# Layer 2's second value sweep: two of eight one-hots and the weight copy on GpSimd

## The chip, the cores and the metric

One Trainium2 chip; the kernel is one program on one core. The metric is device time in microseconds: 5602.24 us, the median of 3 runs (5601.0 to 5603.31).

## What is computed

Four graph layers run on 3125 nodes of 128 features and 50000 edges that are sorted by target. The change touches the third one (its code name is L2), and there only the last step of its second attention convolution. Cut to that:

```python
alpha = jnp.einsum('ehc,ehc->eh', q[dst], k[src]) / jnp.sqrt(jnp.float32(C))   # H=2 heads, C=128
p = jnp.exp(alpha - amax[dst])
denom = jax.ops.segment_sum(p, dst, num_segments=n) + 1e-16
out = jax.ops.segment_sum(p[:, :, None] * v[src], dst, num_segments=n)
out = out / denom[:, :, None]
out = out.mean(axis=1)          # mean of the two heads
return out + x @ Ws + bs
```

The softmax weights are known before the step begins (`alpha` in the kernel holds weight over denominator, halved for the mean). So each edge e has to add alpha[e,0] * v0[src] + alpha[e,1] * v1[src] to the row of its target node.

## The kernel before

Edges lie in tiles of 128, one edge to a partition. There are T = 416 tiles; each belongs to one block of 128 target nodes. Eight tiles (HU = 8) make a half, four halves (S4 = 4) an iteration, 13 iterations (G) a sweep: 52 halves. `half_no(i, h)` numbers them, m in what follows. `each_half` runs a function over all halves inside a loop of 13 iterations on one engine.

The sum over edges is a matmul: for each tile a one-hot matrix (128 edges by 128 nodes, 1 where the edge's target is that node) is the weight operand, the 128 mixed value rows are the moving operand, and the product is added to the node block's place in PSUM. `rec[1][:, tile, 1]` holds each edge's target inside its block, `iota_f` the numbers 0 to 127; comparing the two gives the one-hot.

The sweep is called L2F, "values mixed". Its data is already in DRAM, in the order of the edges (`rows_v2`, two heads side by side, 256 floats an edge). Each engine runs its own program, tied by counting semaphores:

- SyncE, `values_in` (L607 to L611): when a quarter of the ring is free (`ring_free`, given by TensorE), it issues one 1 MB transfer of eight tiles into `ring256`. Four halves fit in the ring.
- VectorE, `mix` (L1475 to L1487): copies the two softmax weights of the half's edges into `relw` (L1480), multiplies head 1's values by their weight (L1482), makes the eight one-hots in one instruction of 128x1024 into one of two slots of `ohv` (L1484, shown by the profile as L965, the helper's line), and adds head 0's scaled values (L1487). The one-hots of half m wait until TensorE is done with half m-2, whose slot they take; the add waits for ScalarE.
- ScalarE, `scale_l2f` (L1712 to L1720): waits for the weights in `relw`, then scales head 0's values tile by tile, eight instructions a half.
- TensorE, `sums_f` (L2143 to L2153): loads eight block numbers into registers, waits for the one-hots and the mixed values, runs eight fp32 matmuls (each two records in the trace), waits for its own last one, and frees the quarter of the ring.
- GpSimd does nothing in this sweep. Ahead of it lie the gathers of the scores' sweep (L2D), behind it those of the last layer (L3), which wait for node rows that are written after the sweep.

The names in the change: `gate(s, n)` is GpSimd's wait, with one increment of a helper semaphore; `last_head` (L784 on) is a function of L2's first value sweep, L2C, in which GpSimd already makes a part of the one-hots, with `tensor_scalar` on 128x128 (L793), after two small copies into `relw` (L780, L781). VectorE's work in L2C is a one-hot instruction of 128x1024 a half (L965 again), products of 128x256 (L1366) and sums that read PSUM (L1378). Elsewhere in the kernel, in the sort of the edges, GpSimd's small copies (L674, L675) run beside VectorE's comparisons L860 and L851.

Of the kernel before, what the change touches and what calls it, by code (L numbers as in the profile page):

```python
# [25 lines left out]
def gnn_stack(nc, a, out):  # L26
    f32, bf16, i32 = mybir.dt.float32, mybir.dt.bfloat16, mybir.dt.int32
    ALU, ACT, AX = mybir.AluOpType, mybir.ActivationFunctionType, mybir.AxisListType.X
    ds = bass.ds
    x_in, src_in, dst_in, w_in = a["x"], a["src"], a["dst"], a["edge_weight"]  # L30

    P, F = 128, 128
# [21 lines left out]
    NG = J // HU  # L54
    NS = 5
    JQ = J // 4
    assert 0 < EP <= P and P * JM + EP * HU == E and CH * CB == NB and NG % NS == 0 and NG % 2 == 0 and G * U >= (E + NB * (P - 1)) // P

    ctx = ExitStack()
    with ctx:  # L60
# [272 lines left out]
        def ph(name):  # L333
            if name not in made:
                made[name] = sem(name)
            return made[name]
# [29 lines left out]
        def half_no(i, h):  # L366
            return i * S4 + h
# [39 lines left out]
        def tiles_of(i, h):  # L407
            return ds(i * U + h * HU, HU)

        def each_half(eng, half):  # L410

            with eng.Fori(0, G) as i:
                for h in range(S4):
                    half(i, h)
# [228 lines left out]
        def _(pool):  # L643
# [16 lines left out]
            def gate(s, n):  # L660
                pool.wait_ge(s, n)
                pool.sem_inc(s_gate, 1)
# [138 lines left out]
                last_head(G - 1, h, (G - 1, h + 1) if h < S4 - 1 else None)  # L801
            gate(ph("node_rows"), ROWS["n2b"] + 16 * CH)
            gathers("L2D", 1, t_kv, 512, None)
            gate(ph("node_rows"), ROWS["n3"] + 16 * CH)
            gathers("L3", 1, t_h3, F, ring)

        @block.vector
        def _(dve):
# [666 lines left out]
            def mix(i, h):  # L1475

                s = h % 2
                m = half_no(i, h)
                v = ring256[:, h * HU:(h + 1) * HU, F:2 * F]
                V.tensor_copy(relw[:, s, :, 1:3], alpha[:, tiles_of(i, h), 0:2]).then_inc(ph("L2F_weights"), 1)  # L1480
                dve.wait_ge(s_rows[h], values_reloaded(i, h))
                V.tensor_tensor(v, v, alpha[:, tiles_of(i, h), 1:2].to_broadcast([P, HU, F]), ALU.mult).then_inc(ph("L2F_mixed"), 1)  # L1482
                dve.wait_ge(ph("L2F_product"), m + 1)
                one_hots(ohv[:, s * HU:(s + 1) * HU, :], 1, i, h).then_inc(ph("L2F_onehot"), 1)  # L1484
                dve.wait_ge(ph("L2F_mixed"), 2 * m + 1)
                dve.wait_ge(ph("L2F_scaled"), m * HU + HU)
                V.tensor_tensor(v, v, ring256[:, h * HU:(h + 1) * HU, 0:F], ALU.add).then_inc(ph("L2F_mixed"), 1)  # L1487

            each_half(dve, mix)
# [40 lines left out]
        def _(act):  # L1530
# [181 lines left out]
            def scale_l2f(i, h):  # L1712

                s = h % 2
                m = half_no(i, h)
                act.wait_ge(ph("L2F_weights"), m + 1)
                act.wait_ge(s_rows[h], values_reloaded(i, h))
                for k in range(HU):
                    v = ring256[:, h * HU + k, 0:F]
                    A.activation(v, v, ACT.Copy, scale=relw[:, s, k, 1:2]).then_inc(ph("L2F_scaled"), 1)  # L1720

            each_half(act, scale_l2f)

            root("n3")
# [13 lines left out]
        def _(pe):  # L1738
# [404 lines left out]
            def sums_f(i, h):  # L2143
                m = half_no(i, h)
                blocks = blocks_of(1, i, h)
                pe.wait_ge(ph("L2F_onehot"), m + 1)
                pe.wait_ge(ph("L2F_mixed"), 2 * m + 2)
                for k in range(HU):
                    last = M.matmul(psum_blocks[:, ds(blocks[k], 1), :], ohv[:, (h % 2) * HU + k, :],  # L2149
                                    ring256[:, h * HU + k, F:2 * F].unsqueeze(1), start=False, stop=False)  # L2150
                last.then_inc(ph("L2F_product"), 1)
                pe.wait_ge(ph("L2F_product"), m + 3)
                pe.sem_inc(ph("ring_free"), 1)  # L2153
# [58 lines left out]
```

## Time and profile before

| | |
|---|---|
| median of 3 runs | 5602.24 us |
| lowest, highest | 5601.0, 5603.31 us |
| the profiled execution | 5603.99 us |
| its span, first to last instruction | 5602.3 us |
| mean granted TensorE clock | 0.726 |
| busy, whole kernel: TensorE, VectorE, ScalarE, GpSimd | 3034.5, 3058.7, 961.0, 3701.8 us |
| the sweep L2F | about 4787 to 4999 us after the start, 212 us |

The profile shows for each engine when it was busy and what released it from a wait. A granted clock of 1.00 is 2.4 GHz and 0.50 is 1.2 GHz; a value between is a mean over a stretch. Only the sweep L2F is changed, so the views below are of that stretch, and of the places where the added kind of work already runs.

### The profile page before, as it was taken

Reading aid. Unit: us, or ns where it says so; the run is one execution under the profiler, and the core shown is the slowest. Engines: PE = TensorE matmul, PEld = TensorE weight load, DVE = VectorE, ACT = ScalarE, POOL = GpSimd, SP = SyncE. Lnnn points to the kernel's source line nnn. Section 1 sums busy time; section 2 is a strip of 40 time slices with the busy share of each in tenths; the row PEclk is TensorE's granted clock in tenths of the full one; section 3 lists DMA queues with packets and bytes.
Section 4 is the critical chain, followed back from the end, with each engine's and each line's share of the span. In section 5 each row is a group of like instructions: output and inputs, shape, how many; then the busy total and the mean of one; then the engine's idle time right before and its main releaser. Section 6 shows DMA issues by size and latency. Waiting matters only on the chain.

```text
span 5602.3 us, 75577 instructions
## 1 busy us (share of the span) xinstructions
PE 3034.5 (54%) x17159; PEld 2186.4 (39%) x17160; DVE 3058.7 (55%) x6436; ACT 961.0 (17%) x3599; POOL 3701.8 (66%) x4254
## 2 busy tenths in 40 slices
PE   3443377753333660144457776688896665544334
PEld 2333266653333660143433332233354433443333
DVE  9888622232223684133349888888516666881111
ACT  1121000000001000000015554577400000550000
POOL 1788777767777777777747775577416776007775
PEclk9999955555555555555579999899997777776556
DMA  2212112221112670133334444122128999552222
GB/s 56 67 27 53 52 52 52 52 42 26 27 26 16 102 107 13 37 82 80 81 59 129 130 128 122 38 60 60 32 87 266 342 330 309 197 173 53 52 52 52
DMA packets 292233, 520.85 MB, mean 93 GB/s; under 512 B 88170, under 2 KB 161120, under 8 KB 285408
## 3 DMA queue, kind: packets, MB, share of 16 engines
q1 hardware_dynamic: 166440, 284.29, 17.9%
q0 software_dynamic: 125728, 235.82, 17.2%
q8 instruction: 26, 0.43, 0.0%
q14 instruction: 39, 0.32, 0.0%
HBM read 418.05 MB, written 101.80 MB: 93 GB/s over the span
## 4 chain that ended last, share of the span: by engine, by line
POOL 45%; issue 30%; DVE 11%; PE 8%; DVEq 2%; ACT 2%; DMA 1%; POOLq 1%; ACTq 0%; SPq 0%; PEldq 0%
POOL work L719 30%; POOL rec_by_dst L679 6%; POOL rec_by_src L679 4%; PE ps L2086 3%; DVE acc L1378 3%; POOL acc L719 2%; POOL idx_slot L713 1%; ACT work L1720 1%; PE ps L1883 1%; PE ps L2149 1%; PE ps L2124 1%; PE ps L2073 1%; DVE work L860 1%; DVEq L403 1%; DVE work L909 1%
## 5 line engine op out<-in xcount | busy, mean ns | idle before, releaser
L1823 PE MATMUL ps<-work 128*128 128x128 f32 (+1 forms) x2496 | 705.0, 445 | 681.6 <-DMA work<-t_v,idx_slot 354.3
L719 POOL DMA_INDIRECT work<-t_h,idx_slot x832 | 799.0, 960 | 240.1 <-issue 221.7
L719 POOL DMA_INDIRECT work<-t_v,idx_slot x832 | 789.8, 949 | 240.1 <-issue 221.6
L1823 PEld LDWEIGHTS ps<-work 128*128 128x128 f32 x2496 | 587.1, 330 | 705.4 <-issue 705.4
L679 POOL DMA_INDIRECT rec_by_src<-sc_rec_s,sc_idx x392 | 420.8, 1074 | 113.3 <-issue 104.2
L719 POOL DMA_INDIRECT work<-t_xl,idx_slot x416 | 413.0, 993 | 120.1 <-issue 111.0
L679 POOL DMA_INDIRECT rec_by_dst<-sc_rec_d,sc_idx x392 | 396.4, 1011 | 113.3 <-issue 104.6
L2051 PE MATMUL ps<-big,work 128*128 x832 | 389.6, 611 | 126.9 <-DVE work L1320 126.0
L2073 PE MATMUL ps<-work 128*128 128x512 f32 x832 | 390.2, 609 | 73.4 <-DVE work L1366 48.3
L2124 PE MATMUL ps<-big,work 128*128 x832 | 324.0, 548 | 194.5 <-DVE aS L1435 123.1
L975 DVE COPY relw<-rec_s 128x16 f32 x104 | 19.4, 186 | 723.6 <-PE ps L1823 723.1
L713 POOL COPY idx_slot<-rec_d 128x8 int32 (+1 forms) x208 | 47.0, 226 | 528.7 <-DMA t_h<-acc 359.3
L793 POOL TENSOR_SCALAR work<-iota_f,relw 128x128 f32<-128x128 f32 x312 | 306.0, 985 | 123.2 <-PE ps L2073 113.9
L1684 ACT ACTIVATE work<-work,relw 128x128 f32<-128x128 bf16 x1040 | 326.5, 389 | 133.8 <-DVE work L965 69.4
L2124 PEld LDWEIGHTS ps<-big,work 128*128 128x128 f32 x832 | 208.6, 270 | 309.6 <-issue 275.8
L1378 DVE TENSOR_TENSOR acc<-acc,ps 128x512 f32 x416 | 284.5, 684 | 47.0 <-DVE acc L1378 44.5
L2006 PE MATMUL ps<-work 128*128 128x128 f32 x832 | 196.1, 430 | 208.6 <-DVE work L1269 208.6
L1320 DVE TENSOR_TENSOR work<-ps,work 128x512 f32<-128x512 f32 x416 | 279.6, 683 | 51.2 <-DMA work<-t_h,idx_slot 47.7
L965 DVE TENSOR_TENSOR work<-rec_d,ps 128x1024 f32<-128x1024 f32 x52 | 63.4, 1222 | 433.6 <-PE ps L1823 433.0
L1822 PEld LDWEIGHTS ps<-one_column,work 128*128 128x128 f32 x832 | 224.9, 330 | 173.3 <-issue 173.3
L1667 ACT ACTIVATE work<-work 128x128 f32<-128x128 f32 x832 | 250.1, 301 | 243.1 <-DVE work L1320 243.1
L965 DVE TENSOR_TENSOR work<-rec_d,iota_f 128x1024 f32<-128x1024 f32 (+1 forms) x156 | 190.7, 1222 | 177.3 <-PE ps L2006 167.6
(415 smaller groups left out, 6589.8 us busy)
## 6 DMA issues: line engine op xcount, KB each, us to landing
work<-rows_of_v_by_position SPq DMA_DIRECT2D x52, 1024.0 KB
work<-relT_by_dst SPq DMA_DIRECT2D x156, 256.0 KB
rows_of_h_by_position<-work SPq DMA_DIRECT2D x52, 512.0 KB
work<-rows_of_h_by_position SPq DMA_DIRECT2D x52, 512.0 KB
rows_of_v_by_position<-work SPq DMA_DIRECT2D x26, 1024.0 KB
rows_of_v_by_position<-acc SPq DMA_DIRECT2D x26, 1024.0 KB
work<-t_v,idx_slot POOLq DMA_INDIRECT x832
work<-relT_by_src SPq DMA_DIRECT2D x52, 256.0 KB
```

The costliest lines, as they stand in the source:

```text
L679: nc.gpsimd.indirect_dma_start(rec_dram[o], bass.IndirectOffsetOnAxis(ap=sc_idx[:, h * HU + k:h * HU + k + 1], axis=0), sc_rec[o][:, h * H ...
L719: nc.gpsimd.indirect_dma_start(to, None, table, bass.IndirectOffsetOnAxis(ap=idx_slot[:, h * HU + k:h * HU + k + 1], axis=0)).then_inc(s_g ...
L793: nc.gpsimd.tensor_scalar(ohw[:, k % 4, 3 * P:4 * P], iota_f[:, :], relw[:, s, k, 0:1], relw[:, s, k, 4:5], ALU.is_equal, ALU.mult).then_i ...
L965: return V.tensor_tensor(out_t, rec[o][:, tiles_of(i, h), 1:2].to_broadcast([P, HU, P]), iota.unsqueeze(1).to_broadcast([P, HU, P]), ALU.i ...
L1320: V.tensor_tensor(prod[:, k % 4, :].rearrange("p (h c) -> p h c", h=4), q, g, ALU.mult).then_inc(sig("L2A", "_multiplied"), 1)
L1378: V.tensor_tensor(part, part, ps[:, k % 4, :].unsqueeze(1), ALU.add).then_inc(ph("L2C_added"), 1)
L1667: ins = A.activation(q, q, ACT.Copy, accum_out=aS[:, s * HU + k, hd:hd + 1])
L1684: ins = A.activation(ohw[:, k % 4, hd * P:(hd + 1) * P], ohm[:, s * HU + k, :], ACT.Copy, scale=relw[:, s, k, 1 + hd:2 + hd])
L1823: ins = M.matmul(psum_blocks[:, ds(b, 1), 0:width], oh[:, s, :], ring[:, h * HU + k, 0:width].unsqueeze(1), start=False, stop=False)
L2051: M.matmul(ps[:, k % 4, :].unsqueeze(1), ohT[:, s, k * P:(k + 1) * P], big[:, ds(blocks[k], 1), :], start=True, stop=True).then_inc(sig("L ...
L2073: M.matmul(ps[:, k % 4, :], ring[:, h * HU + k, :], ohw[:, k % 4, :], start=True, stop=True).then_inc(ph("L2C_product"), 1)
L2124: last = M.matmul(ps[:, k % 4, 0:256].unsqueeze(1), ohT[:, s, k * P:(k + 1) * P], q2[:, ds(blocks[k], 1), :], start=True, stop=True)
```

## The change

GpSimd gets a loop of its own for the sweep. Per half it copies the softmax weights of the next half into `relw[..., 1:3]` and two columns of target numbers into `relw[..., 0:1]`, once ScalarE is done with the half before and its own one-hots are done; then it makes the half's last two one-hots (tiles 6 and 7) one by one. VectorE no longer copies the weights and makes six one-hots instead of eight. TensorE waits for both. Two engines give themselves credits at the start, and the counts of the waits are shifted to match.

```diff
+    FEWER = HU - 2
...
+            def weights_l2f(i, h):
+                s = h % 2
+                nc.gpsimd.tensor_copy(relw[:, s, :, 1:3], alpha[:, tiles_of(i, h), 0:2]).then_inc(ph("L2F_weights"), 1)
+                nc.gpsimd.tensor_copy(relw[:, s, FEWER:HU, 0:1], rec[1][:, ds(i * U + h * HU + FEWER, HU - FEWER), 1:2]).then_inc(ph("L2F_weights"), 1)
+
+            def last_one_hots(i, h, nxt):
+                s = h % 2
+                m = half_no(i, h)
+                if nxt:
+                    gate(ph("L2F_scaled"), m * HU + HU)
+                    gate(ph("L2F_helped"), m * (HU - FEWER) + HU - FEWER)
+                    weights_l2f(*nxt)
+                gate(ph("L2F_weights"), m * 2 + 2)
+                gate(ph("L2F_product"), m + 1)
+                for k in range(FEWER, HU):
+                    nc.gpsimd.tensor_scalar(ohv[:, s * HU + k, :], iota_f[:, :], relw[:, s, k, 0:1], None, ALU.is_equal).then_inc(ph("L2F_helped"), 1)
+
+            gate(ph("sm_back"), 6)
+            pool.sem_inc(ph("L2F_helped"), HU - FEWER)
+            weights_l2f(0, 0)
+            with pool.Fori(0, G - 1) as i:
+                for h in range(S4):
+                    last_one_hots(i, h, (i, h + 1) if h < S4 - 1 else (i + 1, 0))
+            for h in range(S4):
+                last_one_hots(G - 1, h, (G - 1, h + 1) if h < S4 - 1 else None)
...
-                V.tensor_copy(relw[:, s, :, 1:3], alpha[:, tiles_of(i, h), 0:2]).then_inc(ph("L2F_weights"), 1)
...
-                one_hots(ohv[:, s * HU:(s + 1) * HU, :], 1, i, h).then_inc(ph("L2F_onehot"), 1)
+                V.tensor_tensor(ohv[:, s * HU:s * HU + FEWER, :], rec[1][:, ds(i * U + h * HU, FEWER), 1:2].to_broadcast([P, FEWER, P]),
+                                iota_f[:, :].unsqueeze(1).to_broadcast([P, FEWER, P]), ALU.is_equal).then_inc(ph("L2F_onehot"), 1)
...
-                dve.wait_ge(ph("L2F_scaled"), m * HU + HU)
+                dve.wait_ge(ph("L2F_scaled"), m * HU + 2 * HU)
...
-                act.wait_ge(ph("L2F_weights"), m + 1)
+                act.wait_ge(ph("L2F_weights"), m * 2 + 2)
...
+            act.sem_inc(ph("L2F_scaled"), HU)
...
                 pe.wait_ge(ph("L2F_onehot"), m + 1)
+                pe.wait_ge(ph("L2F_helped"), (m + 2) * (HU - FEWER))
                 pe.wait_ge(ph("L2F_mixed"), 2 * m + 2)
```

## Rows read from the trace of the kernel before

**Rows 1.** The page's busy tenths, 40 slices of 140 us; VectorE.

```profile
DVE  9888622232223684133349888888516666881111
```

**Rows 2.** Stretches: us, busy us of each engine, clock, DMA share, GB/s.

```profile
4787.00:4999.00 212.00, 130.99 (x840) 117.76 (x841) 186.33 (x208) 128.49 (x417) 0.00 (x0) 0.85 0.70 238
5100.00:5200.00 100.00, 36.48 (x158) 33.90 (x158) 12.22 (x10) 0.00 (x0) 77.31 (x90) 0.64 0.20 52
4849.00:4871.00 22.00, 12.28 (x96) 11.17 (x96) 20.47 (x24) 13.12 (x43) 0.00 (x0) 1.00 0.88 292
4907.00:4912.00 5.00, 3.52 (x17) 3.24 (x17) 4.21 (x5) 3.62 (x13) 0.00 (x0) 0.50 0.65 234
```

**Rows 3.** TensorE in order of time: start, duration, what, idle before and releaser.

```profile
4852.93 2.05 PE L2149 MATMUL ps<-work 128*128 128x128 f32 x16 [1.43 <-issue]
4856.84 2.05 PE L2149 MATMUL ps<-work 128*128 128x128 f32 x16 [1.86 <-issue]
...
4909.01 3.78 PE L2149 MATMUL ps<-work 128*128 128x128 f32 x16 [1.48 <-DVE work L965]
4914.19 2.05 PE L2149 MATMUL ps<-work 128*128 128x128 f32 x16 [1.41 <-DVE work L965]
```

**Rows 4.** VectorE in order of time, in the same stretch.

```profile
4909.02 1.23 DVE L1487 TENSOR_TENSOR work<-work 128x1024 f32<-128x1024 f32 x1
...
4912.94 1.23 DVE L965 TENSOR_TENSOR work<-rec_d,iota_f 128x1024 f32<-128x1024 f32 x1 [1.48 <-PE ps L2149]
4914.08 1.22 DVE L1487 TENSOR_TENSOR work<-work 128x1024 f32<-128x1024 f32 x1
4915.22 0.17 DVE L1480 COPY relw<-alpha 128x16 f32 x1
4915.30 1.22 DVE L1482 TENSOR_TENSOR work<-work,alpha 128x1024 f32<-128x1024 f32 x1
```

**Rows 5.** Groups by line, 4787 to 4999: busy us, mean ns, idle before, releasers.

```profile
L2149 PE MATMUL ps<-work 128*128 128x128 f32 x832 | 128.0, 317 | 80.6 <-DVE work L965 26.7 <-issue 24.3 <-DVE work L1482 23.1
L1720 ACT ACTIVATE work<-work,relw 128x128 f32<-128x128 f32 x416 | 127.2, 388 | 79.9 <-DVE relw L1480 79.9
...
L1487 DVE TENSOR_TENSOR work<-work 128x1024 f32<-128x1024 f32 x52 | 63.7, 1224 | 12.1 <-ACT work L1720 11.9
...
L1480 DVE COPY relw<-alpha 128x16 f32 x52 | 9.0, 172 | 1.5 <-ACT alpha L1630 1.5
```

**Rows 6.** GpSimd in L2C: its group by line, and the start in order of time.

```profile
L793 POOL TENSOR_SCALAR work<-iota_f,relw 128x128 f32<-128x128 f32 x312 | 306.0, 985 | 123.2 <-PE ps L2073 113.9 <-POOL relw L781 0.4
...
3540.87 0.20 POOL L780 COPY relw<-rec_d 128x8 f32<-128x8 f32 x1 [6.53 <-ACT alpha L1630]
3541.01 0.20 POOL L781 COPY relw<-alpha 128x32 f32<-128x32 f32 x1
...
3541.61 1.59 POOL L793 TENSOR_SCALAR work<-iota_f,relw 128x128 f32<-128x128 f32 x2 [0.40 <-POOL relw L781]
```

**Rows 7.** Order of time at three places where both engines read SBUF.

```profile
359.02 1.28 DVE L860 TENSOR_TENSOR work<-big,iota_f 128x1024 bf16<-128x1024 f32 x1
359.67 0.68 POOL L674 COPY sc_idx<-big 128x8 int32 x1
360.23 0.36 DVE L851 TENSOR_TENSOR work<-big 128x200 bf16<-128x200 f32 x1
...
3629.93 1.22 DVE L965 TENSOR_TENSOR work<-rec_d,iota_f 128x1024 bf16<-128x1024 f32 x1
3630.04 1.77 POOL L793 TENSOR_SCALAR work<-iota_f,relw 128x128 f32<-128x128 f32 x1
...
3634.55 0.79 POOL L793 TENSOR_SCALAR work<-iota_f,relw 128x128 f32<-128x128 f32 x1 [1.35 <-PE ps L2073]
...
3634.95 0.43 DVE L1366 TENSOR_TENSOR work<-work,relw 128x256 f32<-128x256 bf16 x1 [0.44 <-issue]
```

**Rows 8.** ScalarE's first scalings of the sweep.

```profile
4787.52 2.45 ACT L1720 ACTIVATE work<-work,relw 128x128 f32<-128x128 f32 x8 [0.63 <-DVE relw L1480]
```

## The prediction

> **What bounds the kernel now.** I read the busy tenths first: the sweep lies in the 35th and 36th slice, where VectorE shows 8 both times [rows 1]. That suggests VectorE as the bound. The table by stretches makes it exact: in the 212 us of the changed sweep VectorE is busy 186, TensorE 131, ScalarE 128, GpSimd 0, at a mean granted clock of 0.85 [rows 2]. The clock takes two levels here (1.00 and 0.50, that is 2.4 and 1.2 GHz), so 0.85 means about 30% of the stage at the lower one. The next view is TensorE in order of time. A half's 16 matmul records (8 fp32 matmuls) take 2.05 us at 1.00 and up to 3.78 at 0.50, and ahead of each half TensorE idles 1.41 to 1.48 us, every fourth time 1.86 [rows 3]. That gap is the key. At 4914.19 TensorE starts a half whose VectorE add ran from 4909.02 to 4910.25, and at 4912.94 VectorE itself had waited 1.48 us for TensorE [rows 3, 4]. So the gap is not a wait for data: TensorE waits for its own last matmul, loads eight block numbers (every fourth time after a loop branch) and only then asks for its operands. TensorE's least time for the stage is then its busy 128.0 us plus 13 x (1.41 + 1.41 + 1.43 + 1.86) = 79.4 us of gaps, and it shows 80.6 us of idle time [rows 3, 5]: some 1.2 us in 212 are waits for VectorE or ScalarE. **TensorE's own loop bounds the sweep**, 3.58 us a half at the full clock (2.05 + 79.4/52) and 5.2 to 5.3 at the lower. (128.0 - 52 x 2.05) / 1.73 gives 12.4 halves at 1.2 GHz and 39.6 at 2.4. VectorE is second: three instructions 1.14 us apart, the copy 0.08, and some 0.3 waiting for ScalarE (11.9 us in 40 times), 3.8 in all [rows 4, 5]. It takes longer than TensorE where the clock is 2.4 GHz and catches up where it is 1.2, as at 4912.94, where it waits for TensorE.
>
> **What the change takes from VectorE.** The copy of the weights goes: 0.172 us long, but the next instruction starts 0.08 after it [rows 4, 5]. The one-hots shrink from 128x1024 to 128x768. A 128x256 product (L1366) takes 0.43 us and the 128x1024 one-hots 1.22 [rows 7], so 256 elements are 0.26: 1.14 becomes 0.88 from start to start. ScalarE's weights no longer wait for VectorE's previous half, so the wait of 0.3 ahead of L1487 [rows 5] can go. VectorE falls from 3.8 to 1.14 + 0.88 + 1.14 = 3.16 a half. On the path this is worth only the share of the 1.2 us in which TensorE waits, since its 52 gaps stay: I book nothing. ScalarE's eight scalings (2.45 us a half [rows 8]) stay; its 79.9 us of idle time [rows 5] sits beside TensorE's loop.
>
> **What it gives to GpSimd.** Each half now has two small copies and two one-hots there. The same forms exist in L2C: copies of 0.20 us, 0.14 apart, then 0.40 to the first one-hot, and two one-hots in 1.59 [rows 6]. From the last one-hot to the next copies there are two more waits on semaphores, one of them for its own one-hots; no row has them, and between 0.1 and 0.4 (the nearest wait of that kind [rows 6]) I take 0.3. Alone, a half costs GpSimd 0.14 + 0.20 + 0.40 + 1.59 + 0.3 = 2.6 us, which TensorE's 3.58 would hide.
>
> It is not alone. A GpSimd one-hot that starts 0.11 us after VectorE's one-hots (L965, both inputs in SBUF) takes 1.77 us, against 0.79 for one that meets no such instruction at its start [rows 7]: it stands still until about 1.09 us after the start of VectorE's instruction. The mean over the 312 is 985 ns, although L2C's half has one such long instruction to six one-hots, for most of VectorE's work there (L1378) reads PSUM [rows 6]. Small copies stretch too: one takes 0.68 us behind L860, where one alone takes 0.20 [rows 6, 7]. VectorE gives up nearly nothing: that L860 takes 1.28 us, L965 of the same shape 1.22 [rows 7]. In this sweep all three VectorE instructions read twice from SBUF and stand back to back. They would cover 3.16 us of each half, the state in which a one-hot stands still.
>
> **GpSimd's time a half.** Lower bound 2.6, none blocked. If each of the four once stands behind a full instruction: one-hots 2 x 1.77, copies 2 x 0.68, the waits between them 0.7, 5.6. For the value between: with a half of T us, 3.16/T of it is covered, and a start inside waits 0.57 on average (half of 1.14), so T = 2.6 + 4 x 0.57 x 3.16/T, which gives T = 4.3. I take 4.3: in L2C, where fewer instructions block, blocked and free one-hots already mix (312 at 985 ns), and here blocking is denser. TensorE starts a half only with both GpSimd one-hots there, so halves at 2.4 GHz go from 3.58 to 4.3: 39.6 x 0.72 = +28 us. Those at 1.2 GHz (5.2) hide 4.3 and let GpSimd get ahead, 12 x 0.9 = 11 us at most; it can run only two halves ahead (two slots), so I take -8. The larger gap makes TensorE idler, and idler stretches have the lower clock: with TensorE busy 36% the clock is 0.64 in the sweep L3, with 62% it is 0.85 here [rows 2]. At 4.3 it would be busy some 55%. I let the halves at 1.2 GHz grow from 12 to 21: 9 x (5.2 - 4.3) = +8. Its bounds are 0 and 20 more of them, 0 to +18.
>
> **The other added parts.** ScalarE's first weights come from two GpSimd copies that start together with VectorE's first product instead of one VectorE copy ahead of it (scaling starts at 4787.52 [rows 8]): each copy behind one instruction, 1.3 + 1.1 at most, nothing at least; +2. ScalarE's later waits for weights have scalings queued behind them, for which only VectorE's add waits; the weights of a half are written one half early, so they are late only when GpSimd is. Behind TensorE's new wait stand the eight matmuls and the credit that frees a quarter of the ring, so the reloads of 1 MB start later. No DMA is added or moved; the reloads keep 0.88 of the DMA engines busy at TensorE's fastest pace [rows 2], and a slower pace relaxes that. GpSimd's queue holds nothing else until the gathers of L3, which wait for node rows made after the sweep. Two credits (one instruction each on ScalarE and GpSimd) are nothing.
>
> **A rule weighed against the rows.** VectorE's instruction that starts 0.40 us into a GpSimd one-hot is not held up: 0.43 us long, the one-hot 0.79 [rows 7]. So GpSimd seems to need the reading path only early in its instruction, and VectorE pays at most the 0.06 of L860. The Trainium skill, SBUF — State Buffer, "Who interferes with whom", says otherwise for this side: whichever of the two starts first has the shared pair for its whole instruction and the other stands still. It also says that a two-input VectorE instruction in SBUF contends with GpSimd's reads, which rows 7 bear out. By the first rule the engines would take turns, rival three.
>
> **Rivals.** (1) *Hidden, not slower.* GpSimd's waits fall where VectorE idles anyway: its three instructions fill 3.16 of at least 3.58 us. If GpSimd needs under 3.6 us a half on average (at most two of the four blocked, and briefly), TensorE's loop stays the bound: 5602 + 2 for the start - 1 for waits saved = 5603, give or take 7 for where the clock falls. For it: GpSimd works two halves ahead, and the stretches at 1.2 GHz refill that lead. Against: both engines are released by the same event, TensorE's end two halves back, and VectorE then runs three instructions in a row. It decides at 3.6 us. (2) *Starved.* No row shows a one-hot behind two such instructions in a row. If the 0.05 us between them is too short for its read of 128 elements, each one-hot waits for VectorE's next idle time: GpSimd's half is 3.16 + 1.59 + 0.7 = 5.4 us, TensorE's gaps grow by 1.8 at 2.4 GHz, 39.6 x 1.8 = +71, at 1.2 GHz +2, in all 5675. For it: the 0.68 us copy ended 0.12 after the next VectorE instruction began, so a small read just fits in between [rows 7]; one of 128 elements is larger. (3) *Turns.* GpSimd holds the path for its whole 0.79 us and VectorE waits: 3.16 + 1.59 + 0.34 = 5.1 a half, 52 x 5.1 = 265 for 128.0 + 80.6 = 209, +56: 5658. Against: the overlap at 3634.95 without delay. (4) *Faster.* TensorE's waits vanish and the clock stays up: at most 21.4 us (128.0 - 106.6) and the 1.2, 5580. Against: its gaps do not change. (5) *The change does nothing on its terms*, because GpSimd's one-hots come late in one iteration only; this is rival 1 with another name and has its time.
>
> **How the numbers follow.** The profiled execution took 5603.99 us with a span of 5602.3, the median of three is 5602.24; the sum of terms, 28 - 8 + 8 + 2 = +30, goes on the median: 5632. Chances: forecast (4.0 to 4.9 us a half, 5615 to 5655) 0.50; hidden 0.24; starved 0.15; turns 0.07; faster 0.04. A difference of 0.2%, 11 us, is about what a measurement of this kernel can tell from no change. So faster 0.04, same 0.24, slower 0.72. The range reaches from 5600, inside the hidden case, to 5664, which holds turns and the milder part of starved, and leaves out some 0.2. The likeliest case alone spans 5615 to 5655.
>
> **What would show it.** In the changed profile: GpSimd's one-hots between 0.79 and 1.8 us with a mean over 1.1; TensorE's gaps ahead of L2149's successor over 1.5 us and put down to GpSimd; VectorE's three instructions still 1.22, 0.95 and 1.22 long, with its idle time in waits for TensorE; a granted clock under 0.85 in the sweep; ScalarE's 80 us of waits for VectorE gone. A mean one-hot near 0.8 and gaps of 1.38 to 1.86 as before would prove the hidden case; VectorE's instructions stretched to 1.6 and more, turns; one-hots of over 2 us, starved. The prediction is wrong, too, if TensorE's gap turns out to have been a wait for VectorE after all: then the sweep shortens.

## The result, and the profile after

| | kernel before | changed kernel |
|---|---|---|
| median of 6 runs | 5602.77 us | 5626.39 us |
| lowest, highest | 5595.10, 5608.13 us | 5621.21, 5628.80 us |
| the profiled execution, its span | 5603.99, 5602.3 us | 5627.29, 5625.3 us |
| sweep, VectorE's first product to TensorE's last matmul | 211.1 us | 231.8 us |

The ratio is 1.0039, 95% interval 1.0028 to 1.005: by the ratio the change makes the kernel slower by 22 us, and the medians lie 23.6 us apart. The spans of the two profiled executions differ by 23.0 us. Of these 20.7 lie in the sweep, and 2.2 had gathered before it began (VectorE starts it at 4789.7 in place of 4787.4, and nothing ahead of it was changed).

First the sweep by line, as [rows 5] for the kernel before. Columns: busy us, mean ns of one, idle time before them, and what ended it.

```profile
L821 POOL TENSOR_SCALAR work<-iota_f,relw 128x128 f32<-128x128 f32 x104 | 147.3, 1425 | 12.4 <-PE ps L2178 11.9
L2178 PE MATMUL ps<-work 128*128 128x128 f32 x832 | 141.3, 339 | 87.9 <-DVE work L1510 60.4 <-POOL work L821 26.0 <-issue 1.5
...
L1747 ACT ACTIVATE work<-work,relw 128x128 f32<-128x128 f32 x416 | 126.2, 388 | 97.6 <-POOL relw L809 70.5 <-DMA work<-rows_of_v_by_position 27.1
L1508 DVE TENSOR_TENSOR work<-work,alpha 128x1024 f32<-128x1024 f32 x52 | 64.9, 1247 | 1.6 <-ACT alpha L1657 1.6
L1514 DVE TENSOR_TENSOR work<-work 128x1024 f32<-128x1024 f32 x52 | 64.1, 1232 | 4.5 <-ACT work L1747 3.7
L1510 DVE TENSOR_TENSOR work<-rec_d,iota_f 128x768 f32<-128x768 f32 x52 | 49.9, 959 | 50.6 <-PE ps L2178 50.6
L809 POOL COPY relw<-rec_d 128x2 f32 x48 | 32.7, 680 | 0.0
L808 POOL COPY relw<-alpha 128x16 f32 x48 | 21.3, 443 | 12.9 <-POOL work L821 12.3 <-issue 0.3 <-ACT work L1747 0.3
```

VectorE's one-hots fell from 1.22 to 0.96 us and its copy is gone, but it now idles 50.6 us for TensorE. TensorE (L2178 is the former L2149) shows both parts of the loss: 13.3 us more of matmuls, though they are the same 832, and 7 us more of idle time. The stretch by itself (us, busy us of TensorE, its weight loads, VectorE, ScalarE and GpSimd, then clock, DMA share, GB/s), against 0.85 for the clock in [rows 2]:

```profile
4789.00:5023.00 234.00, 144.78 (x843) 131.01 (x846) 171.90 (x156) 127.70 (x418) 202.30 (x208) 0.78 0.63 215
```

GpSimd, idle before, is now the busiest engine of the stage. TensorE in order of time, first its start and then one iteration of four halves (start, duration, what, idle before and what ended it):

```profile
4794.27 2.05 PE L2178 MATMUL ps<-work 128*128 128x128 f32 x16 [2.01 <-POOL work L821]
4800.73 3.77 PE L2178 MATMUL ps<-work 128*128 128x128 f32 x16 [4.41 <-POOL work L821]
...
4849.71 2.96 PE L2178 MATMUL ps<-work 128*128 128x128 f32 x16 [2.00 <-POOL work L821]
4854.14 3.62 PE L2178 MATMUL ps<-work 128*128 128x128 f32 x16 [1.48 <-DVE work L1510]
4859.27 2.05 PE L2178 MATMUL ps<-work 128*128 128x128 f32 x16 [1.50 <-DVE work L1510]
4862.79 2.05 PE L2178 MATMUL ps<-work 128*128 128x128 f32 x16 [1.48 <-DVE work L1510]
4866.84 3.01 PE L2178 MATMUL ps<-work 128*128 128x128 f32 x16 [2.00 <-POOL work L821]
```

One gap is a plain wait for GpSimd: 4.41 us ahead of the second half, where the kernel before has 1.78. The rest of the sweep looks almost as before. In an iteration's steady state the kernel before has gaps of about 1.49, 1.39, 1.41 and 1.88 us, the changed kernel of 1.50, 1.49, 1.50 and 1.98: three of the four are longer by 0.1, one is as it was. Only at halves 38 and 42 (counted from 0) is there another wait for GpSimd, of 0.35. The 26.0 us that the group puts down to GpSimd (12 times) are mostly TensorE's own loop, as at 4849.71, where e_wait below, without GpSimd, has the same 2.0; GpSimd's one-hots merely were the last operand to come. They came with little to spare, though: eight halves start only 0.4 us after GpSimd's last one-hot, and 0.24 is what it takes where TensorE really waits. What changed from iteration to iteration is the time of the matmuls. From one iteration's first matmul to the next one's, the kernel before takes 16.5 to 16.9 us eight times, 17.5 at the start and 14.3 to 14.4 in three iterations without a single half at 1.2 GHz. The changed kernel has 21.1 at the start, 19.3 once and 17.0 to 17.5 in the others: no iteration without halves at 1.2 GHz is left. TensorE's clock is at 1.2 GHz for 101.9 us of the sweep, before for 64.1.

GpSimd in order of time, first its second pair of one-hots and then two pairs that stand one iteration apart:

```profile
4795.76 4.73 POOL L821 TENSOR_SCALAR work<-iota_f,relw 128x128 f32<-128x128 f32 x2
...
4851.33 1.17 POOL L821 TENSOR_SCALAR work<-iota_f,relw 128x128 f32<-128x128 f32 x2
...
4868.50 1.17 POOL L821 TENSOR_SCALAR work<-iota_f,relw 128x128 f32<-128x128 f32 x2
```

And the view of that line: number, then shortest, median and longest in ns. One by one, 33 of the 104 took 0.6 us, 42 from 1.1 to 1.7 and 29 from 2.1 to 2.7.

```profile
L821 POOL TENSOR_SCALAR work<-iota_f,relw x104: 593/1328/2713, 4791.8 to 5017.0; 128x128 f32<-128x128 f32 x104
```

### The profile page after: what moved, and what is told of

Read it like the earlier page. It is cut to its first block, busy times and chain, and to the rows that moved or that the text cites. A ratio compares the mean times of both kernels' runs of the same rounds, so it can differ in the third digit from the quotient of the medians.

```text
span 5625.3 us, 76185 instructions
## 1 busy us (share of the span) xinstructions
PE 3049.1 (54%) x17150; PEld 2191.0 (39%) x17160; DVE 3041.6 (54%) x6384; ACT 960.1 (17%) x3599; POOL 3904.3 (69%) x4462
## 4 chain that ended last, share of the span: by engine, by line
POOL 46%; issue 30%; DVE 11%; PE 8%; DVEq 2%; DMA 2%; POOLq 1%; ACT 1%; SPq 0%; PEldq 0%; ACTq 0%
POOL work L720 30%; POOL rec_by_dst L680 6%; POOL rec_by_src L680 4%; PE ps L2114 3%; DVE acc L1405 3%; POOL acc L720 2%; PE ps L2178 2%; POOL idx_slot L714 1%; PE ps L1911 1%; POOL work L821 1%; DVE work L887 1%; PE ps L2101 1%; DVEq L404 1%; DVE work L936 1%; PE ps L2152 0%
## 5 line engine op out<-in xcount | busy, mean ns | idle before, releaser
L2079 PE MATMUL ps<-big,work 128*128 x832 | 390.9, 613 | 127.8 <-DVE work L1347 126.9
L2152 PEld LDWEIGHTS ps<-big,work 128*128 128x128 f32 x832 | 200.1, 263 | 314.5 <-issue 286.3
L2079 PEld LDWEIGHTS ps<-big,work 128*128 128x128 f32 x832 | 151.0, 191 | 329.6 <-issue 319.5
L1005 DVE TENSOR_SCALAR work<-ps,relw 128x128 f32<-128x128 f32 x832 | 274.3, 401 | 3.8
```

Source lines behind the costliest of these rows:

```text
L1005: last = V.tensor_scalar(oh[:, s * HU + k, :], iota_p, relw[:, s, k, 0:1], relw[:, s, k, 1:2], ALU.is_equal, ALU.mult)
L2079: M.matmul(ps[:, k % 4, :].unsqueeze(1), ohT[:, s, k * P:(k + 1) * P], big[:, ds(blocks[k], 1), :], start=True, stop=True).then_inc(sig("L ...
L2152: last = M.matmul(ps[:, k % 4, 0:256].unsqueeze(1), ohT[:, s, k * P:(k + 1) * P], q2[:, ds(blocks[k], 1), :], start=True, stop=True)
```

## Experiments

The kernels e_six, e_side, e_wait, e_side_wait, e_dvewait, e_one, e_again and e_early_one ran on two other chips, where the kernel before takes 7037 and 6988 us because other stages take longer; each ratio is to the kernel before on the same chip, and the sweep itself has its usual length there: on the first of them 210.7 and 210.4 us in e_side and e_six, against 211.1, on the second 232.8 in e_again, against 231.8. The table gives the sweep as above, the busy time of TensorE's matmuls, the 51 gaps between its halves, and the time in the sweep at 1.2 GHz. (What the sweep has beyond matmuls and gaps is the way to the first matmul, 3.9 to 4.7 us.) The ratio is of whole kernels over several executions. The other columns come from one profiled execution each; the repeat e_again is 1.0 us from the changed kernel, and the three kernels that hardly touch the sweep are within 1.0 us of the kernel before, so differences of 1 or 2 us tell nothing.

| kernel | ratio, 95% interval | sweep us | matmuls | gaps | at 1.2 GHz |
|---|---|---|---|---|---|
| before | | 211.1 | 128.0 | 79.1 | 64.1 |
| changed | 1.0039 [1.0028, 1.0050] | 231.8 | 141.3 | 85.9 | 101.9 |
| e_again | 1.0035 [1.0019, 1.0051] | 232.8 | 141.6 | 86.5 | 106.5 |
| e_six | 1.0003 [0.9992, 1.0015] | 210.4 | 127.6 | 78.9 | 63.0 |
| e_weights | 1.0001 [0.9992, 1.0010] | 212.1 | 129.7 | 78.5 | 68.4 |
| e_side | 0.9997 [0.9985, 1.0008] | 210.7 | 127.1 | 79.7 | 64.5 |
| e_wait | 1.0009 [1.0000, 1.0018] | 220.2 | 132.1 | 84.2 | 76.2 |
| e_side_wait | 1.0010 [0.9999, 1.0020] | 222.7 | 134.4 | 84.4 | 82.6 |
| e_one | 1.0021 [1.0009, 1.0032] | 222.3 | 134.1 | 84.1 | 81.5 |
| e_dvewait | 1.0030 [1.0019, 1.0041] | 227.7 | 139.4 | 83.5 | 98.1 |
| e_early | 0.9986 [0.9977, 0.9995] | 205.0 | 126.0 | 75.1 | 54.7 |
| e_early_after | 1.0032 [1.0020, 1.0044] | 225.9 | 134.3 | 87.0 | 79.6 |
| e_early_one | 0.9980 [0.9968, 0.9991] | 199.4 | 127.8 | 67.4 | 58.2 |
| e_early_weights | 0.9948 [0.9934, 0.9961] | 179.7 | 106.5 | 69.3 | 3.2 |

**Is VectorE's relief worth nothing?** e_six takes a quarter of VectorE's comparing away and gives it to nobody: VectorE makes six one-hots a half, and tiles 6 and 7 use one-hots made once ahead of the sweep, so a quarter of this step's sums is left out. e_weights moves only the copy of the weights to GpSimd, without a new wait on TensorE.

```diff
-                one_hots(ohv[:, s * HU:(s + 1) * HU, :], 1, i, h).then_inc(ph("L2F_onehot"), 1)
+                V.tensor_tensor(ohv[:, s * HU:s * HU + HU - 2, :], rec[1][:, ds(i * U + h * HU, HU - 2), 1:2].to_broadcast([P, HU - 2, P]),
+                                iota_f[:, :].unsqueeze(1).to_broadcast([P, HU - 2, P]), ALU.is_equal).then_inc(ph("L2F_onehot"), 1)
```

> The kernel before with VectorE making six one-hots a half instead of eight; the last two tiles of each half use one-hots made once before the sweep, so a quarter of this step's sums is left out. VectorE is relieved by 0.27 us a half at no cost. Both theories: TensorE's loop is the bound, so nothing is gained, -2 to +3 us (+2.3 us of it the two instructions ahead of the sweep). If VectorE were the bound after all, 52 x 0.27 = 14 us would go.

> The kernel before, of the change only the copy of the weights on GpSimd: VectorE makes all eight one-hots, TensorE has no new wait. Both theories: TensorE's gaps stay 1.38 to 1.48 us, ScalarE starts 0.3 us earlier, nothing on the path but the start (0 to 1.3 us): sweep 210 to 214 us.

The sweep stays at 210.4 and 212.1 us, with the same gaps. In e_six VectorE's idle time for TensorE is 12.8 us ahead of the shorter one-hots, and TensorE's is what it was [rows 5]:

```profile
L2153 PE MATMUL ps<-work 128*128 128x128 f32 x832 | 127.6, 316 | 82.7 <-DVE work L1484 44.6 <-DVE work L1482 19.9 <-DVE work L1488 15.3
...
L1484 DVE TENSOR_TENSOR work<-rec_d,iota_f 128x768 f32<-128x768 f32 x52 | 49.7, 955 | 12.8 <-PE ps L2153 12.8
```

**What do the change's parts cost one by one?** e_wait adds to the kernel before one wait that is always met. e_side lets GpSimd do all of the change's copies and one-hots into buffers that nothing reads. e_side_wait has both.

```diff
                 pe.wait_ge(ph("L2F_onehot"), m + 1)
+                pe.wait_ge(ph("L2F_weights"), m + 1)
                 pe.wait_ge(ph("L2F_mixed"), 2 * m + 2)
```

> The kernel before with one thing added: TensorE waits once more per half, for a count that has long been reached. No work moves. Theory L (TensorE's own loop): the changed kernel lost its time because this wait lengthens each of TensorE's 52 gaps from about 1.39 to 1.48 us (4.6 us in all) and the idler TensorE gets the lower clock more often (13 us): here both come back, gaps 1.47 to 1.50, sweep 226 to 231 us for 211, kernel +12 to +20 us. Theory P (GpSimd's one-hots come late): a wait that is always met costs its issue alone, at most +5 us, and the granted clock in the sweep stays 0.85.

> The kernel before, and GpSimd does all of the change's work beside it on its own buffers: two copies and two one-hots a half, paced by the same waits, that nobody uses. VectorE keeps its copy and all eight one-hots; TensorE waits for nothing new. Theory L: GpSimd's reads lengthen VectorE's instructions by 0.02 to 0.05 us, VectorE goes from 3.8 to at most 4.0 us a half, TensorE's gaps stay 1.38 to 1.48: between 0 and +6 us. Theory P in its strong form (the two engines take turns on the reading path): VectorE loses over 1 us a half, +50 us. GpSimd's one-hots should take 1.4 us or more on average.

> The kernel before, with both side parts of the change and without its dependence: GpSimd does the change's copies and two one-hots a half into buffers that nothing reads, and TensorE has one more wait, which is always met when it is asked. VectorE's own work is that of before. The added wait alone lengthened the sweep from 211.1 to 220.2 us, GpSimd's side work alone left it at 210.7, the change has 231.8. Theory P (what is missing is GpSimd's lateness, for which TensorE really waits): the two parts don't add up to more than the wait, sweep 218 to 223 us, gaps ahead of TensorE's halves 1.49 to 1.55, ratio 1.0005 to 1.0025. Theory W (the longer wait and the contention together push the stage over, by the clock; lateness is not needed): sweep 228 to 233 us, low clock near 100 us, ratio 1.003 to 1.005.

```profile
L822 POOL TENSOR_SCALAR work<-iota_f,relx 128x128 f32<-128x128 f32 x104 | 108.7, 1054 | 0.5 <-POOL work L822 0.4 <-PE ps L2178 0.2
L1510 DVE TENSOR_TENSOR work<-work,alpha 128x1024 f32<-128x1024 f32 x52 | 67.7, 1302 | 0.1
```

Those are GpSimd's one-hots and VectorE's products in e_side: GpSimd's work alone costs the sweep nothing, for VectorE pays 0.08 us a product (1.302 for 1.219) and it has that to spare. The one-hots took 1.05 us on average there and not the 1.4 or more that I had expected. The wait alone costs 9.1 us: 5.1 of gaps (0.10 a half) and 4.1 of longer matmuls. These are two of TensorE's gaps in e_wait, an ordinary one and one with the loop's branch:

```profile
6201.31 2.05 PE L2150 MATMUL ps<-work 128*128 128x128 f32 x16 [1.50 <-DVE work L965]
6205.36 3.12 PE L2150 MATMUL ps<-work 128*128 128x128 f32 x16 [2.01 <-DVE work L965]
```

Neither of my two theories had that price: one put 15 us and more on the sweep, the other at most 5 with an unchanged clock. With both it is 11.6, which is less than the change's 20.7; the 2.5 between them is hardly more than the spread of a repeat. The whole kernels are too coarse here: the intervals of e_wait and e_side_wait reach to no change at all and up to 13 or 14 us. About 9 us are left, which come only when TensorE also depends on GpSimd's one-hots. Of these, 3.3 are the late start (0.7 to the first matmul, 2.6 to the second half).

**Does GpSimd's lateness count without the third wait?** e_dvewait takes the wait for GpSimd's one-hots from TensorE and puts it ahead of VectorE's add, which TensorE waits for anyway. e_one keeps TensorE's wait and lets GpSimd make one one-hot a half (`FEWER = HU - 1`). e_again is the changed kernel once more.

```diff
-                pe.wait_ge(ph("L2F_helped"), (m + 2) * (HU - FEWER))
...
                 dve.wait_ge(ph("L2F_scaled"), m * HU + 2 * HU)
+                dve.wait_ge(ph("L2F_helped"), (m + 2) * (HU - FEWER))
```

> The changed kernel with one wait moved: VectorE waits for GpSimd's two one-hots ahead of its add, so that TensorE needs no third wait (the add's count covers it). Theory L: TensorE's gaps return to 1.38 to 1.48 us, the granted clock in the sweep to about 0.85, and only the start (3 us) stays: 5603 to 5609 us. Theory P: GpSimd's one-hots come as late as before and now also hold up VectorE's add and with it GpSimd's and TensorE's next half: 5626 us or more.

> The changed kernel with one GpSimd one-hot a half in place of two; VectorE makes seven. TensorE's third wait stays, VectorE's one-hots take about 1.09 us. GpSimd's half falls by one one-hot of 0.59 alone, 1.43 in the company of VectorE, so to some 2.0 alone and 2.9 in company, under TensorE's 3.6. Theory P (wait and lateness each count): lateness is gone, what stays is the wait, sweep 218 to 224 us, ratio 1.0005 to 1.003. Theory W (the wait and the presence of GpSimd's work, whatever its length): sweep 228 to 233, ratio 1.003 to 1.005. By neither does the kernel get faster than before.

> The changed kernel once more, as a second sample of its sweep. The first profile had a sweep of 231.8 us with 101.9 us at the low clock. If that is the stage's usual state: 228 to 234 us again, 95 to 105 us at the low clock, ratio 1.003 to 1.005. If the low clock there was an accident of one execution (theory C: the 13 us of longer matmuls are chance and not caused), a sweep of 218 to 226 us in this profile.

In e_dvewait TensorE's gaps are back at 1.38 to 1.50 in most places, and still the sweep takes 227.7 us: VectorE and GpSimd fell into one cycle, shown here by GpSimd, and then by VectorE's add in the same stretch.

```profile
6198.69 1.90 POOL L821 TENSOR_SCALAR work<-iota_f,relw 128x128 f32<-128x128 f32 x2
6200.86 1.05 POOL L808 COPY relw<-alpha 128x16 f32 x1 [0.27 <-POOL work L821]
6201.84 1.19 POOL L809 COPY relw<-rec_d 128x2 f32 x1
6203.00 1.90 POOL L821 TENSOR_SCALAR work<-iota_f,relw 128x128 f32<-128x128 f32 x2
```

```profile
6200.62 1.23 DVE L1515 TENSOR_TENSOR work<-work 128x1024 f32<-128x1024 f32 x1 [1.08 <-POOL work L821]
6201.77 1.22 DVE L1508 TENSOR_TENSOR work<-work,alpha 128x1024 f32<-128x1024 f32 x1
6202.91 0.95 DVE L1510 TENSOR_TENSOR work<-rec_d,iota_f 128x768 f32<-128x768 f32 x1
6204.94 1.23 DVE L1515 TENSOR_TENSOR work<-work 128x1024 f32<-128x1024 f32 x1 [1.08 <-ACT work L1748]
```

A half costs GpSimd 6203.00 - 6198.69 = 4.31 us there. Each copy ends with a VectorE instruction (6201.91 after 6201.85, 6203.03 after 6202.99), and of each pair of one-hots the first, beside VectorE's own, takes 1.3 and the second 0.6. So an explanation by the third wait alone falls. e_one is the counterpart: it keeps that wait, and its sweep is that of e_side_wait (222.3 against 222.7), so with one one-hot GpSimd's lateness is gone and the cost of the wait and of the company stays: once the start is over, TensorE begins every half 2.3 us or more after GpSimd's one-hot. The range came true although GpSimd's single one-hot took 2.49 us on average and not the 1.43 behind it. e_again confirms the changed kernel's stage with 232.8 us; its 106.5 us at 1.2 GHz are even above the 95 to 105 expected, so the low clock is no accident of one execution.

**What sets the pace once TensorE's loop is shorter?** In e_early and its three relatives TensorE loads the next half's block numbers while its matmuls run, and waits for its product and frees the ring one half later; SyncE's count for the ring is raised by one to match.

```diff
+                pe.wait_ge(ph("L2F_product"), m + 2)
+                pe.sem_inc(ph("ring_free"), 1)
                 pe.wait_ge(ph("L2F_onehot"), m + 1)
...
                 last.then_inc(ph("L2F_product"), 1)
-                pe.wait_ge(ph("L2F_product"), m + 3)
-                pe.sem_inc(ph("ring_free"), 1)
```

> The kernel before with TensorE's loop reordered: the eight block numbers of the next half are loaded while the matmuls of this one still run, and only then does TensorE wait for its last matmul and free the ring. This takes away most of the gap that both theories name as the bound. Theory L: the gap falls from 1.4 to under 0.6 us, VectorE's 3.8 us a half becomes the bound, TensorE idles evenly and keeps the upper clock (0.95 or more), sweep 52 x 3.8 = 198 us and a little, 12 us less than 211. If TensorE's gap was a wait for data after all, nothing changes.

> The changed kernel with the same reordering. Now nothing of TensorE's covers GpSimd's half. Theory P: GpSimd needs 4.3 us a half or more beside VectorE (its copies and one-hots each stand behind VectorE's instructions), so the sweep stays at 224 us or more, TensorE put down as waiting for GpSimd. Theory L: GpSimd keeps up with VectorE's 3.2 us a half, and the change pays off once the loop is short: sweep 175 to 190 us, under that of the reordered kernel before.

> That copy on GpSimd together with the reordered loop of TensorE. VectorE is the bound and has three instructions 1.14 us apart and no wait for ScalarE, 3.42 to 3.6 us a half, with TensorE's 2.05 us and a short gap hidden: sweep 180 to 190 us at the upper clock, 20 to 30 us less than the kernel before. If GpSimd's one small copy a half holds up ScalarE behind VectorE's instructions, it stays near the 198 of the reordered kernel.

> The changed kernel with one GpSimd one-hot a half, and TensorE's loop reordered (the next half's block numbers are loaded while the matmuls run, and the ring's credit is given after the product one half later). With two one-hots and this order GpSimd set the pace at 4.34 us a half (225.9 us for 52, TensorE waiting 78.0 us for it); with none of them, but the weights' copy on GpSimd, VectorE set it at 3.46 (179.7 us). With one, GpSimd needs 4.34 - 1.46 = 2.9 us, less than VectorE, which needs 1.14 + 1.01 + 1.14 = 3.29. Theory P (GpSimd's pace is a sum of its instructions with their blocking): VectorE stays the bound, sweep 172 to 184 us, ratio 0.993 to 0.996. Theory S (a one-hot gets its turn only when VectorE idles, so one is about as bad as two): sweep 200 to 226 us, ratio 0.998 to 1.003.

The reordering alone gave 6 us of the 13 that were expected (205.0 us, where I had 198): TensorE then waits for VectorE, which waits 15.3 us for ScalarE, whose weights VectorE copies. With the change on top GpSimd is the bound, at 225.9 / 52 = 4.34 us a half: TensorE waits for it 36 times, 78.0 us in all. With only the weights' copy on GpSimd the sweep takes 179.7 us (180 to 190 expected), the kernel 5573.77 us against 5604.76 beside it, ratio 0.9948: faster than both kernels. Its rows by line, and TensorE in order of time:

```profile
L1737 ACT ACTIVATE work<-work,relw 128x128 f32<-128x128 f32 x416 | 126.9, 388 | 47.3 <-DMA work<-rows_of_v_by_position 46.8 <-POOL relw L807 0.5
L2169 PE MATMUL ps<-work 128*128 128x128 f32 x832 | 106.5, 281 | 70.6 <-DVE work L1504 70.6
...
L1504 DVE TENSOR_TENSOR work<-work 128x1024 f32<-128x1024 f32 x52 | 62.9, 1210 | 0.2 <-ACT work L1737 0.2
```

```profile
4851.99 2.05 PE L2169 MATMUL ps<-work 128*128 128x128 f32 x16 [1.35 <-DVE work L1504]
4855.39 2.05 PE L2169 MATMUL ps<-work 128*128 128x128 f32 x16 [1.36 <-DVE work L1504]
4858.80 2.05 PE L2169 MATMUL ps<-work 128*128 128x128 f32 x16 [1.36 <-DVE work L1504]
```

VectorE is the bound, three instructions of 1.135 us from start to start, and from the first matmul on the clock stays at 2.4 GHz. Of the 25.3 us by which the sweep is shorter than in e_early, 19.5 are the matmuls' (126.0 to 106.5): most of the gain is the clock, and 5.8 are gaps. That order would have made room for the change's own idea, and e_early_one tried it with one one-hot. It missed its range: 199.4 us, where I had 172 to 184. That is next to the 200 to 226 of the other theory, in which one one-hot is about as bad as two. GpSimd's single one-hot takes 1.94 us there, not 1.43.

```profile
L2180 PE MATMUL ps<-work 128*128 128x128 f32 x832 | 127.8, 317 | 69.0 <-POOL work L821 57.5 <-PE ps L2180 6.0 <-DVE work L1514 5.4
...
L821 POOL TENSOR_SCALAR work<-iota_f,relw 128x128 f32<-128x128 f32 x52 | 101.0, 1942 | 5.0 <-PE ps L2180 4.6 <-POOL relw L809 0.5
...
L809 POOL COPY relw<-rec_d 128x1 f32 x48 | 42.6, 888 | 0.0
L808 POOL COPY relw<-alpha 128x16 f32 x48 | 31.2, 649 | 15.5 <-POOL work L821 8.5 <-ACT work L1747 6.7 <-issue 0.3
```

A half costs GpSimd 0.65 + 0.89 + 1.94 = 3.48 us and 0.39 of idle time (20.5 us in 52 halves), about the sweep's 3.83 a half, and TensorE waits 57.5 us for it: with one one-hot it is still the bound. 31 of the 52 took 2.3 us and more. The mean of 1.43 came from pairs, of which one is mostly short.

## Why the prediction came out as it did

**TensorE's loop as the bound.** Right, and now shown: e_six and e_weights relieve VectorE and gain nothing; e_early shortens the loop and gains 6 us in the sweep and 9 in the kernel.

**The relief of VectorE at nothing, its 0.26 and the vanished waits.** Right: 0.959 us in place of 1.22, and ScalarE waits for the reloads or GpSimd instead of VectorE. What I did not see is that relief has a value once TensorE's loop is shorter: e_early_weights, which moves the copy alone, takes 5573.77 us against the 5595.84 of e_early, 22 us less.

**GpSimd's half, 2.6 alone and 4.3 beside VectorE.** The size was right where GpSimd sets the pace: 4.31 us in e_dvewait, together with VectorE, and 4.34 in e_early_after. In the changed kernel it repeats every 17.17 / 4 = 4.29 us (one-hots that start at 4851.33 and again at 4868.50), but that proves nothing: in e_wait, where GpSimd does nothing, eight of the twelve iterations of TensorE take 17.1 to 17.3 us too. The model behind the size was not right: the one-hot alone is shorter (0.593 us at the least; I had 0.79 from [rows 6]), and the blocked ones come in two kinds, one of about 1.33 or 1.58 us and one of 2.4 to 2.7. Which kind it is depends on VectorE's next instruction. Of the 104 one-hots, 33 start while no VectorE instruction runs and take 0.59 to 0.61 us. For 40 the running VectorE instruction ends 0.02 us or more before the next one starts: they take 1.13 to 1.58. For 31 the next one starts before the running one has ended, and 29 of these take over 2.1. In e_again it is 30, 42 and 32, with 30 over 2.1. The two errors of the model cancelled, which is luck: for one one-hot a half the same model was wrong (2.49 us in e_one).

**+28 for gaps that grow from 3.58 to 4.3 a half.** Wrong in place. TensorE's gaps grew by only 6.7 us in all. Of these the start is 2.6, and the other 50 gaps together are 4.1, about 0.08 each. That is the issue of the third wait, which I had priced at nothing and which e_wait shows by itself (gaps +5.1); later waits for GpSimd are 0.7 of it. If GpSimd's pace reached TensorE, it was hardly by waits. An iteration with two halves at 1.2 GHz takes 17.1 us by TensorE's own loop, about GpSimd's time for four halves, so nothing is late in it. What is missing are the iterations of 14.4 us.

**+8 for the clock, -8 for GpSimd's lead.** Mis-sized: matmuls at 1.2 GHz cost 13.3 us more, inside the bounds of 0 to 18 that I gave, and e_again has 13.6. In steps, from the table: the wait alone +4.1, GpSimd's company +2.3 more, TensorE's dependence on GpSimd +6.9 more. My reason for the term, that a stretch in which TensorE is idler has the lower clock, does not hold either: in e_early_weights the matmuls fill 106.5 of 179.7 us, a smaller share than 128.0 of 211.1 in the kernel before, and the clock is the higher one. The lead of GpSimd was never a term of its own.

**+2 for the start.** VectorE's first product to the first matmul took 0.66 us longer, but the second half's one-hots came 2.6 us late: 3.3 instead of 2. I had looked at ScalarE's weights and not at GpSimd's second pair of one-hots, which stood behind four VectorE instructions without a pause (4795.76, 4.73 us for two).

**What would show it.** The one-hots' mean (1.425, over 1.1), VectorE's three durations, its idle time in waits for TensorE, ScalarE's missing waits for VectorE and the lower clock came as listed. The one-hots' range did not: 33 took less than 0.79 us and 29 more than 2, which I had listed as the sign of starved. The sign that carried the largest term, gaps of over 1.5 us put down to GpSimd, did not: the gaps are 1.48 to 1.53, most of them put down to VectorE, and 2.0 every fourth time.

So the sum of +30 is near the measured +22 to +24, and part of that is luck. I had booked 20 us for gaps (28 - 8), 8 for the clock and 2 for the start; by the trace it was 4.1 for gaps after the start, 13.3 for the clock and 3.3 for the start, together 20.7. The sum stands for a floor of 4.3 us a half, and e_early_after shows that floor where TensorE's loop no longer covers it; that it is what acts in the changed kernel is not shown. By cause, from one trace each, it reads: third wait 9.1, GpSimd's company on top 2.5, dependence on GpSimd 9.1 (the start included), together 20.7.

**The rivals.** Hidden falls by its number (5603), but half of it was so: after the start GpSimd is seldom waited for. Starved exists as a form, and not as the pace of the changed kernel. In e_one 49 of the 52 one-hots look like this, with VectorE's two instructions beside it:

```profile
6166.32 2.57 POOL L821 TENSOR_SCALAR work<-iota_f,relw 128x128 f32<-128x128 f32 x1
```

```profile
6166.28 1.09 DVE L1510 TENSOR_TENSOR work<-rec_d,iota_f 128x896 f32<-128x896 f32 x1
6167.29 1.22 DVE L1514 TENSOR_TENSOR work<-work 128x1024 f32<-128x1024 f32 x1
6168.42 1.31 DVE L1508 TENSOR_TENSOR work<-work,alpha 128x1024 f32<-128x1024 f32 x1
```

The one-hot starts 0.04 us into VectorE's one-hots and ends 0.38 after the add that follows, at 6168.89. In the changed kernel, though, only one pair of 52 has two such one-hots (4.73 us); otherwise a long one is followed or preceded by a shorter one, which keeps a pair's two at 2.85 us together on average. Turns falls: in the changed kernel VectorE's instructions took 1.247, 0.959 and 1.232 us on average, and the longest of all 1.37, 0.15 more than alone and far from a whole GpSimd instruction more. So the rule of the Trainium skill, SBUF — State Buffer, "Who interferes with whom", that the engine that comes second stands still for the first one's whole instruction, is borne out for GpSimd (it even stands still over two) and not for VectorE. Faster falls for this change.

**What stays open.** How GpSimd's two one-hots lower TensorE's clock. The count of iterations without any half at 1.2 GHz, of 13, follows one thing: it is 0 in the changed kernel, e_again, e_dvewait and e_early_after, in all of which TensorE depends, by itself or through VectorE's add, on two GpSimd one-hots a half, and at least 1 in every other one (4 in the kernel before, 1 in e_wait, 2 in e_side_wait, 3 in e_one). That is consistent with GpSimd being unable to do four halves in less than about 17.1 us, so that an iteration that starts faster ends in a wait and an idler TensorE. One place in the changed kernel looks like that. Two halves at 1.2 GHz (3.78 us each, the second is the first line here) are followed by three at 2.4 GHz, then TensorE waits 0.35 us for GpSimd (1.83 in place of 1.48), and in that half, number 38, the lower clock is back:

```profile
4945.26 3.78 PE L2178 MATMUL ps<-work 128*128 128x128 f32 x16 [1.48 <-DVE work L1510]
4950.56 2.05 PE L2178 MATMUL ps<-work 128*128 128x128 f32 x16 [1.53 <-DVE work L1510]
4954.57 2.05 PE L2178 MATMUL ps<-work 128*128 128x128 f32 x16 [1.95 <-DVE work L1510]
4958.12 2.05 PE L2178 MATMUL ps<-work 128*128 128x128 f32 x16 [1.50 <-DVE work L1510]
4961.99 2.63 PE L2178 MATMUL ps<-work 128*128 128x128 f32 x16 [1.83 <-POOL work L821]
```

In e_again it goes the same way at half 18. In e_one and e_side_wait, where no such wait comes, two halves of 3.78 us are followed by five at 2.4 GHz, twice in each; in e_dvewait by four, twice, and then by a gap of 2.15 to 2.18 us and the lower clock. These are few places, though, and that GpSimd's pace does it, and not the order in which a half's operands come, was not isolated.

## What to carry to other kernels

Before work is taken off the busiest engine, look at what the gap of the engine behind it consists of: here TensorE's gap was its own waits and register loads, and only after those had been moved under the matmuls was relief for VectorE worth anything (22 us for one small copy, against nothing for the same copy without it), most of it by the clock. Count every semaphore wait that is added to such a loop, met or not. Helper work on GpSimd beside back-to-back VectorE instructions has to be priced at the end of those instructions and not at its own length, and the cheapest piece (here one copy) may be all that pays.

## What was not expected of the hardware

- A wait that is always met costs TensorE's queue 0.10 us a half in e_wait (gaps 84.2 against 79.1 us in 51 gaps), and with the time at 1.2 GHz, which rises from 64.1 to 76.2 us, the sweep is 9.1 us longer, nearly twice that. One trace shows it.
- A GpSimd one-hot of 128x128 that takes 0.593 us undisturbed took 2.1 to 2.713 us in 29 cases of the changed kernel, in all of which VectorE's next instruction started before the one that ran at its start had ended. Where 0.02 us or more lay between the two, it took 1.58 at most (40 cases). VectorE's own grew by 0.15 at most.
- The clock can be given back whole. In e_early_weights the matmuls fill 106.5 of 179.7 us and TensorE is at 2.4 GHz from its first one on (the 3.2 us at 1.2 GHz lie ahead of it). In the kernel before the same matmuls take 128.0 of 211.1 us, with 64.1 us at 1.2 GHz. The halves in e_early_weights are evenly 3.41 us apart; before, every fourth gap is longer by 0.4 to 0.5. Which feature of the gaps makes the difference was not tried.
